# Expert stage of a graph network: first-matrix products of block b+1 ahead of second-matrix products of block b

## What is computed

```python
logits = xt @ Wr + br
probs = softmax(logits, axis=-1)
top_p, top_idx = top_k(probs, 2)
weights = top_p / top_p.sum(axis=-1, keepdims=True)
xn = (xt - mu) * rsqrt(var + 1e-5)
xe = xn[None] * ln_g[:, None, :] + ln_b[:, None, :]
h = gelu(einsum('end,edh->enh', xe, W1) + b1[:, None, :])     # 256 -> 1024
y = einsum('enh,ehd->end', h, W2) + b2[:, None, :]            # 1024 -> 256
out = (weights[:, :, None] * take_along_axis(y, top_idx)).sum(axis=1)
```

## Time and profile before

| what | before |
|---|---|
| median of 3 runs | 3795.33 us (3790.81 to 3797.64) |
| span of the profiled execution | 4365.6 us |
| its mean granted TensorE clock | 0.861 |
| PE busy over the span | 3253.1 us, 75% |
| POOL busy over the span | 2531.6 us, 58% |
| expert stage, first transposes to last products | 1372.06 to about 2284.7 us |

### The profile page before, as it was taken

The page is one execution under the profiler, slowest core; times in us unless marked ns, Lnnn a source line. Parts: engine busy times, 40 slices in busy tenths (PEclk is TensorE's granted clock), DMA queues, the critical chain, the costliest instruction groups (busy, mean ns, idle before and its releaser), DMA issues. The chain is left out here.

```text
span 4365.6 us, 47498 instructions
## 1 busy us (share of the span) xinstructions
PE 3253.1 (75%) x15077; PEld 2484.5 (57%) x15077; DVE 1790.8 (41%) x5335; ACT 1496.2 (34%) x2892; POOL 2531.6 (58%) x2604
## 2 busy tenths in 40 slices
PE   1455565555446989988886798987989868999868
PEld 1344444444335777776764576655666645666547
DVE  4355565534353111111117333343333435676664
ACT  3233333323323112121115244443444434555520
POOL 6666666666643656565546666665666656666620
PEclk6677777777767999999988899988999979999978
DMA  6343334334312545554437454554544534555452
GB/s 194 111 122 109 117 115 118 116 108 120 101 40 98 176 157 179 172 185 156 157 124 269 124 146 136 149 159 116 144 138 142 166 107 143 150 153 152 135 175 103
DMA packets 396972, 609.34 MB, mean 140 GB/s; under 512 B 81648, under 2 KB 295319, under 8 KB 395943
## 3 DMA queue, kind: packets, MB, share of 16 engines
q0 software_dynamic: 115808, 279.40, 22.6%
q1 hardware_dynamic: 274182, 317.02, 22.4%
q10 hardware_dynamic: 6720, 9.74, 0.7%
HBM read 509.58 MB, written 96.33 MB: 139 GB/s over the span
## 5 line engine op out<-in xcount | busy, mean ns | idle before, releaser
L2983 POOL DMA_INDIRECT rows_h<-table,step_src x1138 | 1105.8, 972 | 688.6 <-issue 342.5
L3025 PE MATMUL bank_g<-rows_hl,counts_h 128*128 128x512 f32 x3773 | 1049.8, 422 | 89.0 <-issue 45.4
L975 POOL DMA_INDIRECT rows_r<-table,step_src x782 | 749.6, 959 | 405.2 <-issue 214.1
L3025 PEld LDWEIGHTS bank_g<-rows_hl,counts_h 128*128 128x128 f32 x3773 | 721.3, 194 | 301.9 <-issue 101.0
L1000 PE MATMUL bank_r<-rows_r,hots_r 128*128 128x257 f32 x1564 | 473.4, 457 | 457.4 <-ACT rows_r L985 227.3
L1000 PEld LDWEIGHTS bank_r<-rows_r,hots_r 128*128 128x128 f32 x1564 | 340.1, 227 | 567.6 <-ACT rows_r L985 261.6
L3184 ACT ACTIVATE counts_h<-piece_h 128x896 fp32r<-128x896 uint8 x539 | 498.1, 945 | 458.8 <-PE bank_g L3025 223.3
L1901 POOL DMA_INDIRECT kept_A<-one_d,place_d x424 | 420.7, 992 | 127.4 <-issue 127.1
L2016 PE MATMUL pY_e<-w_e,h_e 128*128 128x256 f32 x1680 | 421.7, 410 | 76.7 <-ACT h_e L1982 54.4
L1011 DVE TENSOR_SCALAR hots_r<-lane,step_dst 128x128 f32<-128x128 f32 x782 | 210.3, 289 | 593.3 <-remote 365.2
L1982 ACT ACTIVATE h_e<-pH_e,prm_e 128x256 f32<-128x256 f32 (+1 forms) x456 | 179.6, 455 | 733.7 <-PE pH_e L2005 486.5
(11 more groups left out here) (397 smaller groups left out, 3864.9 us busy)
## 6 DMA issues: line engine op xcount, KB each, us to landing
w_e<-in_L_ffn_W SPq DMA_DIRECT2D x114, 1024.0 KB
piece_h<-kept_A SPq DMA_DIRECT2D x539, 112.0 KB
kept_A<-zero_r SPq DMA_DIRECT2D x189, 112.0 KB
rows_h<-table,step_src POOLq DMA_INDIRECT x1138
table<-ACC SPq DMA_DIRECT2D x51, 256.0 KB
kept_sw<-vec_g SPq DMA_DIRECT2D x49, 256.0 KB
rows_r<-table,step_src POOLq DMA_INDIRECT x782
b_e<-in_L_ffn_b SPq DMA_DIRECT2D x57, 128.0 KB
```

The source lines that it names most:

```text
L975: nc.gpsimd.indirect_dma_start(out=r["rows"][:, x, 0:D], out_offset=None, in_=r["table"][:, :], in_offset=bass.IndirectOffsetOnAxis(ap=c[" ...
L2983: nc.gpsimd.indirect_dma_start(out=d["rows"][:, x, :], out_offset=None, in_=tables[l - 1][:, :], in_offset=bass.IndirectOffsetOnAxis(ap=c[ ...
L3025: mm = pe.matmul(sums, d["counts"][:, n % CV, x % PC, :], both.both(t), start=(x == 0 and i >= RINGED[l]), stop=(x == NT - 1))
```

## The change

h_e gets two buffers, chosen by b % 2. DVE makes the inputs two blocks ahead instead of one. PE's first products become a function `hidden(b)` which waits, bank by bank, for gelu of block b-1 (before, the wait of the second products for the same gelu had covered this). PE's order becomes: first products of b+1, transposes of b+2, second products of b. POOL, ACT's order and SP are as they were.

```diff
-        h = sb("h_e", [P, HJ, BR], F32, ctx)
+        h = sb("h_e", [P, 2, HJ, BR], F32, ctx)
...
             inputs(0)
+            inputs(1)
             for b in range(NBLK):
-                if b + 1 < NBLK:
-                    inputs(b + 1)
+                if b + 2 < NBLK:
+                    inputs(b + 2)
...
-                        a = act.activation(h[:, k, 0:w], pH[j][:, n * BR:n * BR + w], ACT.Gelu,
+                        a = act.activation(h[:, b % 2, k, 0:w], pH[j][:, n * BR:n * BR + w], ACT.Gelu,
...
-            turn(0)
-            for b in range(NBLK):
+            def hidden(b):
                 q, halves = b % W, block_of(b)[2]
                 pe.wait_ge(s_xe, b + 1)
                 pe.wait_ge(s_w[q], 48 * (b // W + 1))
                 for j in range(HJ // 2):
+                    if b > 0:
+                        pe.wait_ge(s_h, (b - 1) * (HJ // 2) + j + 1)
                     for n in range(2):
                         o = (2 * j + n) * P
                         for k in range(KD):
                             mm = pe.matmul(pH[j][:, n * BR:n * BR + halves * P], w1[:, q, k, o:o + P], xe[:, b % 2, k, 0:halves * P],
                                            start=(k == 0), stop=(k == KD - 1))
                     mm.then_inc(s_mm1, 1)
+
+            turn(0)
+            hidden(0)
+            turn(1)
+            for b in range(NBLK):
+                q, halves = b % W, block_of(b)[2]
                 if b + 1 < NBLK:
-                    turn(b + 1)
+                    hidden(b + 1)
+                if b + 2 < NBLK:
+                    turn(b + 2)
                 if b > 0:
                     pe.wait_ge(s_y, halves_before(b))
                 for j in range(HJ):
                     if j % 2 == 0:
                         pe.wait_ge(s_h, b * (HJ // 2) + j // 2 + 1)
                     for m in range(halves):
-                        mm = pe.matmul(pY[m][:, 0:D], h[:, j, m * P:(m + 1) * P], w2[:, q, j, :],
+                        mm = pe.matmul(pY[m][:, 0:D], h[:, b % 2, j, m * P:(m + 1) * P], w2[:, q, j, :],
                                        start=(j == 0), stop=(j == HJ - 1))
                 mm.then_inc(s_mm2, 1)
```

## The result

The changed kernel takes 4354.69 us (median of 4 runs, 4353.99 to 4356.15) where the kernel before takes 3794.81 us: ratio 1.1475, 95% interval 1.1461 to 1.1488, 560 us slower. 4387 us was forecast, with 4215 to 4540 as the range.

The account below looks back on a forecast made before the run. PE was taken to bound the expert stage at 755 us; the ring through POOL's queue plus clock loss (1009 + 281 + 42 + 14) made it 1346 us, so 3795.3 - 755 + 1346 = 4387 us, range 4215 to 4540.

Parts of the forecast that it names:

- PE bounds the stage: Expert stage before: PE has no idle in an undisturbed block, 14.25 us a whole block, 755 us in a timed run.
- The stalls: Expert stage before: 158 us in some 16 stretches, plus 343 us at later layers' gathers, taken as the profiled execution's.
- The span forecast, 4799 us: Whole changed kernel, against the profiled execution's time: 4365.6 - 912.6 + 1346, stalls mostly fitting into PE's new idle time.
- The ring: Expert stage: second products, results, edges, token gathers, transposes wait in turn; 16.03 us against 6.90 us of work, 9.1 idle.
- POOL's wait: POOL in the expert stage, waiting for y_e: grows from 254.5 us to 650 us or so in total.
- The clock term: PE's transposes and second products after each wait: slower at first, 2.5 us per whole block, 133 us over 53 blocks.
- Weights: First products, one block earlier after the load: load takes 11 us, needed 14.25 us after; fits with 3 us to spare.
- Gelu and the buffers at 0: Expert stage: second half of h_e and first products' wait for the previous block's gelu cost 0, covered by second products.
- The rival with late landings: Token gathers, part of rival 2: each lands 3 us later because edges and weights share DMA engines, 4546 us; rival's chance 0.12.

Follow-up runs that it names:

- The undisturbed profile: The kernel before, unchanged, profiled a second time: 3791.59 us, with a span of 3789.5 us and an expert stage of 769 us.
- the four-ahead kernel: The changed kernel with tokens(b+4) where tokens(b+2) stood, and results of blocks 0 and 1 behind tokens 4 and 5: 3789.44 us, 0.9985 of before.
- The experiment with the gathers first: The changed kernel with tokens(b+2) ahead of the edges of block b on POOL: 4087.15 us, 1.0777 of before.

## Why the prediction was right

- **PE bounds the stage, at 14.25 us a whole block and 755 us in all.** The undisturbed profile has 769 us. The 14 us that were missing are the waits for tokens near single blocks (12.5 us) with the slower products after one of them. The sum had them in neither kernel, and so took the stage before 14 us too short.
- **The stalls belong to the profiled execution.** Right in the main, by the second profile. Both of its supports were too large. The stage was 144 us longer than undisturbed (913 against 769), not 158. The gathers of the later layers have 466 us of idle time on POOL in the undisturbed profile too, against 688.6 in the disturbed one, so 222 us of it were disturbance, not the 343 that the prediction worked out from 1.27 us each. That other waits lie there had not been asked.
- **The span forecast, 4799 us, was wrong.** It kept the disturbance in the rest of the kernel as a fixed part. It is no part of the kernel at all; the 4387 us from the difference of stages was the sum to trust.
- **The ring.** Every step came within 0.1 us: 1.30, 2.61, 1.27 an edge, 1.29, 2.81. The stage was forecast at 1346 us and is 1332. PE was to wait some 9.1 us a whole block, with 6.32 edges on average: it waits 8.58 in the block shown, which has six edges, 9.91 in one with seven, and 466.3 in all. POOL's wait was forecast at about 650 us and is 681.1.
- **The clock term, 2.5 us a block, was too large.** Second products cost 84.5 us more than undisturbed (458.2 less 373.7) and transposes 25.2 (58.4 less 33.2): 110 us, 2.1 a block, against 133. It had been taken near the middle of rows with shorter waits, 1.6 to 3.0 us. This is the term that made the stage of the changed kernel too long. With the stage before too short, the two errors of 14 us added up to 28 of the 32 us by which 4387 is too high. (3795.3 - 755 + 1346 is 4386; the prediction has 1 us more.) The rule of the Trainium skill that stood beside it (TensorE: Matmul & The Clock Gate, "HAM oscillation — how this bites in real kernels") held: nearly every block starts its transposes slowly (1.12 us for four instead of 0.60), the granted clock is 0.83, and filling the wait gave back 91 us.
- **Weights.** Forecast as fitting with 3 us to spare. They fit in the changed kernel, whose blocks are longer. At 14.25 us a block they are late six times, about 6 us in all (the four-ahead kernel). The prediction had not looked at single blocks: with the second products of one in between, the first products come 10.8 us after those that free the buffer (6.91 + 0.44 + 3.46) instead of 14.25, and the load was sized at 11.
- **Gelu and the buffers at 0.** Right: the buffers alone give 1.0003, and the first products of the changed kernel wait 2.3 us in all, for DVE's inputs and never for gelu.
- **The rival with late landings** was put aside for the right reason, that the gathers come after the weights. The experiment with the gathers first shows what it is worth where they don't: 3.1 us a block.

## What to carry to other kernels

When an engine's work is moved ahead, ask for each operand which queue produces it and what stands in front of it there. Here the inputs were asked for a block earlier but the gathers that feed them kept their place behind results of work that now waited for them, and a ring of seven short steps, not the full engine, set the pace. The repair is in the queue that was not touched, and once it is made in both kernels the old order is still the faster one, by 9 us. And a wait that a profile shows is worth removing only if the execution that shows it is like the timed ones: its span against the median tells.

## What the runs showed of the hardware

- An indirect gather of 128 rows of 1 KB lands 2.8 us after its start (median), 5.9 us in the kernel that issues it beside a weight load of 2 MB from SP (2.8 again without the loads).
- One profiled execution of a kernel can be disturbed: 4365.6 us of span against 3789.5 of the next. In its expert stage ACT and DVE stood still for up to 18 us at a time and PE for up to 6.9, while POOL went on. What does this was not found.
- 848 products more made the changed kernel 91 us faster, since PE came out of most waits at the higher clock (granted 0.98 instead of 0.83 in the stage).
